# Three late scatter waits moved, the expert stage ordered by pairs of tiles, and the graph's feed-forward by pairs of tiles

## The chip, the cores and the metric

The kernel runs on one core of a Trainium2 chip. The time is device microseconds from launch to end, the median of 3 runs. The kernel before takes 2256.81 us (2252.81 to 2266.86).

## What is computed

Two layers of a graph network on 1,250 nodes of 512 features and 40,000 edges whose destinations are sorted. The parts that the change touches, cut to their core:

```python
dst = (1250 * uniform(40000) ** 2).astype(int32), sorted        # edges by destination
# graph attention over the edges (scores of every pair of nodes, weighted by a table of edges)
alpha = p / denom[src];  agg = segment_sum(alpha[:, :, None] * v[dst], src)
x = x + agg.reshape(n, C) @ Wo.T + bo
# the graph's feed-forward, 512 -> 1024 -> 512
z = layernorm(x, ln_ff_g, ln_ff_b)
x = x + silu(z @ W1.T + b1) @ W2.T + b2
...
# eight experts, 512 -> 256 -> 512 each, for every node, summed with softmax gates
hid = gelu(einsum('bnd,edf->bnef', y, W1) + b1)
out = einsum('bned,bne->bnd', einsum('bnef,efd->bned', hid, W2) + b2, gate)
```

All data is 32-bit float. A product with float operands shows as two matmul instructions in the trace: a product of 128 rows by 125 columns counts as x2 there.

## The kernel before

The nodes are cut into 10 tiles of 125. Each engine runs its own list of instructions in program order, written out by hand stage by stage (`gnn_...`, `att_...`, `ff_...`, `ffn_...`, `causal_...`, `expert_...`, `l1_...`, `last_...`), and waits on semaphores; a waiting instruction holds up all that stands behind it on its engine. `leave_stage` is a barrier of TensorE (PE), VectorE (DVE) and ScalarE (ACT).

**Edge table and attention.** POOL (GpSimd) scatters the edges into a table in HBM, 313 columns of 128 edges, one indirect DMA per column (L623), two in flight. The attention stage reads the table back in 50 blocks of 125 destinations by 250 sources into three buffers. Blocks 0 to 24 hold the destination tiles 0 to 4, blocks 25 to 49 the tiles 5 to 9: block 25 + 5g + n is destination tile 5 + n for the g-th group of sources. The DMA queue SP issues for each block i, in order: the count store of block i (L223 to adjacency, once ACT has copied the counts, `a_cc`), then the load of block i + 3 (six DMAs at L223 and L224, once DVE has used block i, `a_p`). Before the loads of blocks 25 to 27 it reads the number of scatter columns which the tiles up to that one need (`soon_filled`), and waits for them; before block 28 it waits for all 313 (`table_filled`). DVE multiplies every block by exponentials from ACT in two halves (L1488). The sums of these weights (L1524) are DVE's for blocks 0 to 24; for the later blocks they stand on POOL, behind all scatters. A half-block needs the sum of the half-block three before it, since it takes its buffer.

**Feed-forward (`ff_...`).** Per tile t: DVE normalizes into one buffer (`z`, L192), PE transposes it (`turn`, L198), ACT scales it into columns (`zT`, L1758, 4 activations), PE makes 32 products of 125 columns for the hidden layer (`hidden`, L1797), ACT takes Silu (L1774), PE makes 8 products of 512 columns for the output (`project`, L204, 16 instructions), DVE adds it to x (L1739). PE's order is turn(t + 2), hidden(t + 1), project(t). DVE's list, which the change leaves as it is: z(0), z(1), z(2), then for each tile t two adds (L1734, L1735), z(t + 3), a wait for project(t), the add at L1739, and the statistics of tile t - 1 (L172).

**Experts.** Per tile, PE makes 64 products of 125 columns (L2446) for all eight hidden layers of the next tile, then one bias product (L2473) and 8 x 2 products of 512 columns (L2488) for this tile; ACT takes Gelu of 125 columns at a time (L2413), DVE adds each expert's output times its gate to x (L2394).

Of the kernel before, what the change touches and what calls it, by code (L numbers as in the profile page):

```python
# [15 lines left out]
NODES = 1250  # L16
# [36 lines left out]
def gps_two_layers(nc, d):  # L53
# [11 lines left out]
    with ctx:  # L65
# [562 lines left out]
        SOON_KEYS = [float((SOON_TILES + w) * TP * NODES + 1) for w in range(4)]  # L628
# [776 lines left out]
        def att_sp(sp):  # L1405
# [299 lines left out]
        zT_f = [chunks(space.take(C)) for _ in range(2)]  # L1705
        hT_f = [chunks(space.take(8 * TP), TP, 8) for _ in range(2)]
# [42 lines left out]
        def ff_act(act):  # L1749
# [3 lines left out]
            def zT(t):  # L1753
                act.wait_ge(z_turned, Z_FF + t + 1)
                if t >= 2:
                    act.wait_ge(f_h, 2 * (t - 1))
                for k in range(KC):
                    last = nc.scalar.activation(zT_f[t % 2][:, k, :], bank(t % 2)[:, k * TP:(k + 1) * TP],  # L1758
                                                ACT.Identity, scale=lf_g[:, k:k + 1],
                                                bias=lf_g[:, KC + k:KC + k + 1])  # L1760
# [4 lines left out]
            for t in range(TILES):  # L1765
                if t + 2 < TILES:
                    zT(t + 2)
                if t >= 2:
                    act.wait_ge(f_o, t - 1)
                for a in range(2):  # L1770
                    n = 2 * t + a
                    act.wait_ge(f_h, n + 1)
                    for m in range(4):
                        last = nc.scalar.activation(hT_f[t % 2][:, 4 * a + m, :],  # L1774
                                                    bank(2 + n % 4)[:, m * TP:(m + 1) * TP], ACT.Silu,
                                                    bias=b1_g[:, 4 * a + m:4 * a + m + 1])
                    last.then_inc(f_s, 1)
            leave_stage(act, "ACT")

        def ff_pe(pe):  # L1780
# [8 lines left out]
            def hidden(t):  # L1789
                pe.wait_ge(z_cols, Z_FF + t + 1)  # L1790
                for a in range(2):
                    n = 2 * t + a
                    if n >= 4:
                        pe.wait_ge(f_s, n - 3)
                    for m in range(4):
# [1667 lines left out]
```

## Time and profile before

| | |
|---|---|
| median of 3 runs | 2256.81 us |
| the profiled execution: its time / its span | 2257.32 / 2255.5 us |
| PE busy in the span | 2059.9 us, 91% (DVE 60%, ACT 32%, POOL 32%) |
| chain that ended last, by engine | PE 59%, DVE 17%, DMA 9%, POOL 7%, ACT 4% |
| its lines | L204 17%, table scatters 8% and L623 7%, L2446 6%, L2488 6%, L1797 3% |
| attention from the first late block to its end | 786 to 1006 us |
| feed-forward | 1006 to 1167 us |
| experts | 1547 to 1850 us |

The chain is followed back from the last instruction; what stands in it was waited for. A stage is read by its own rows: who is busy there, who waits, and what ended the wait.

### The profile page before, as it was taken

To read this page: it belongs to the slowest core of one execution; us is meant where nothing else is said; L and a number is where in the kernel's file an instruction comes from. 1 tells how busy PE (TensorE), PEld (TensorE's weight loads), DVE (VectorE), ACT (ScalarE), POOL (GpSimd) and SP (SyncE) were. 2 spreads that over 40 slices of the span, in tenths; PEclk is the share of its full clock that TensorE was granted. 3 is DMA by queue.
4 is the path that set the end of the run, shared out by engine and by line. 5 is a ranking of instruction groups with operands and counts; after the bars stand their busy time and mean duration, and the time that the engine had idled before them with its cause. 6 is when DMAs were issued, how large, how long until landed. Compare 5 with 4: busy or idle time off the path is not lost.

```text
span 2255.5 us, 31449 instructions
## 1 busy us (share of the span) xinstructions
PE 2059.9 (91%) x11986; PEld 1259.6 (56%) x11986; DVE 1352.0 (60%) x3200; ACT 728.0 (32%) x1552; POOL 726.3 (32%) x508
## 2 busy tenths in 40 slices
PE   5998986999999878989999999999999999999977
PEld 3555554443345545547764467678666754455554
DVE  6665687988999967751224543431222243289997
ACT  4221122320035544422223355554111111135553
POOL 1346878887775565430000000000000000024442
PEclk9998998999999989999999999999999999999989
DMA  9995232223449977652000010004000013000000
GB/s 328 386 374 123 3 77 3 3 3 67 63 77 220 213 174 199 182 148 95 1 10 0 1 77 1 1 1 188 1 1 1 1 48 106 1 1 10 10 15 14
DMA packets 122055, 181.99 MB, mean 81 GB/s; under 512 B 67761, under 2 KB 69451, under 8 KB 118071
## 3 DMA queue, kind: packets, MB, share of 16 engines
q1 hardware_dynamic: 76833, 178.51, 25.2%
q0 software_dynamic: 45072, 1.46, 5.7%
q8 instruction: 96, 1.57, 0.3%
q14 instruction: 54, 0.44, 0.1%
HBM read 109.21 MB, written 70.71 MB: 80 GB/s over the span
## 4 chain that ended last, share of the span: by engine, by line
PE 59%; DVE 17%; DMA 9%; POOL 7%; ACT 4%; issue 3%; SPq 1%; DVEq 0%; PEldq 0%; ACTq 0%; POOLq 0%; PEld 0%
PE banks L204 17%; DMA edge_table<-arena 8%; POOL edge_table L623 7%; PE banks L2446 6%; PE banks L2488 6%; PE banks L1797 3%; PE banks L2274 2%; PE banks L2262 2%; PE banks L2249 2%; PE banks L2872 2%; PE banks L1593 2%; PE banks L2298 2%; PE banks L198 2%; PE banks L1614 1%; DVE arena L1488 1%
## 5 line engine op out<-in xcount | busy, mean ns | idle before, releaser
L623 POOL DMA_INDIRECT edge_table<-arena x313 | 521.3, 1666 | 269.4 <-DMA edge_table<-arena 164.5
L204 PE MATMUL banks<-arena 128*125 128x512 f32 x1200 | 550.4, 605 | 15.4 <-DVE arena L3092 14.3
L204 PEld LDWEIGHTS banks<-arena 128*125 128x125 f32 x1200 | 219.5, 191 | 258.2 <-issue 241.1
L2899 POOL CAST arena<-arena 125x128 f32<-125x128 uint32 x10 | 2.9, 290 | 699.3 <-DVE arena L3035 699.3
L1488 DVE TENSOR_TENSOR arena<-banks,arena 125x1000 f32<-125x1000 f32 x100 | 193.3, 1949 | 35.5 <-ACT banks L1567 26.9
L2394 DVE SCALAR_TENSOR_TENSOR arena<-banks,arena 125x512 f32<-125x512 f32 x80 | 60.1, 751 | 189.4 <-PE banks L2488 189.4
L2141 DVE CUSTOM_DVE_ANT_0 arena<-banks,arena 125x512 f32<-125x512 f32 (+8 forms) x144 | 73.0, 553 | 129.1 <-PE banks L2249 126.3
L1593 PE MATMUL banks<-arena 64*125 64x250 f32 x800 | 113.8, 403 | 38.6 <-DVE arena L1488 37.3
L2446 PEld LDWEIGHTS banks<-arena 128*128 128x128 f32 x1280 | 144.0, 192 | 6.7 <-issue 6.6
L2446 PE MATMUL banks<-arena 128*128 128x125 f32 x1280 | 146.4, 276 | 0.1
L1567 ACT ACTIVATE banks<-banks 125x1000 f32<-125x1000 f32 x100 | 99.0, 990 | 139.9 <-PE banks L1599 120.1
L2488 PE MATMUL banks<-arena 128*125 128x512 f32 x320 | 139.2, 593 | 0.0
L1524 POOL TENSOR_TENSOR arena<-arena 125x1000 f32<-125x1000 f32 x40 | 95.8, 2455 | 74.3 <-DVE arena L1488 74.2
L1593 PEld LDWEIGHTS banks<-arena 64*125 64x125 f32 x800 | 69.3, 187 | 79.9 <-DVE arena L1488 58.0
L1197 DVE TENSOR_REDUCE arena<-banks 125x2 f32<-125x1024 f32 (+1 forms) x120 | 112.2, 1029 | 0.0
L1311 PE MATMUL banks<-arena 64*125 64x512 f32 (+1 forms) x480 | 108.4, 555 | 4.0 <-DVE arena L1197 2.5
L2413 ACT ACTIVATE arena<-banks,arena 128x125 f32<-128x125 f32 x160 | 45.2, 369 | 203.1 <-PE banks L2446 203.1
L1614 PE MATMUL banks<-arena 125*64 125x250 f32 x800 | 108.8, 394 | 0.5 <-DVE arena L1488 0.5
L198 PE MATMUL banks<-arena 125*128 125x125 f32 x560 | 83.2, 280 | 23.1 <-DVE arena L753 6.9
L2107 POOL MEMSET arena<- 128x1250 f32 x1 | 1.1, 1140 | 315.9 <-PEq L148 315.9
L2488 PEld LDWEIGHTS banks<-arena 128*125 128x125 f32 x320 | 59.3, 188 | 74.0 <-issue 74.0
L198 PEld LDWEIGHTS banks<-arena 125*128 125x128 f32 x560 | 64.2, 145 | 54.5 <-issue 24.1
(374 smaller groups left out, 3405.9 us busy)
## 6 DMA issues: line engine op xcount, KB each, us to landing
edge_table<-arena SPq DMA_DIRECT2D x23, 2304.0 KB, 24.3
arena<-edge_table SPq DMA_DIRECT2D x100, 326.8 KB
arena<-edge_table SPq DMA_DIRECT2D x50, 330.8 KB
arena<-L_ffn_W SPq DMA_DIRECT2D x4, 2048.0 KB, 10.1
adjacency<-arena SPq DMA_DIRECT2D x50, 109.4 KB
arena<-adjacency SPq DMA_DIRECT2D x10, 546.9 KB
edge_table<-arena POOLq DMA_INDIRECT x313
arena<-edge_table SPq DMA_DIRECT2D x100, 37.9 KB
```

The lines of the kernel that those rows point to most:

```text
L198: last = nc.tensor.transpose(dst[:, k, :], src[:, k * 128:(k + 1) * 128], ident[0:TP, 0:TP])
L204: last = nc.tensor.matmul(dst, xT[:, i, :], w[:, i, 0:n], start=(i == 0), stop=(i == k - 1))
L623: pool.indirect_dma_start(d["table"], bass.IndirectOffsetOnAxis(ap=cell[0:EP, c:c + 1].bitcast(U32), axis=0), vals[0:EP, c * ROW:(c + 1) * ...
L1197: nc.vector.tensor_reduce(by_part_max[:, t, j, :, u % 3], unit_banks(u)[:, :, 0:b - a], AX_X, ALU.max).then_inc(g_mx, 1)
L1311: last = nc.tensor.matmul(unit_banks(u)[:, e, 0:b - a], qT_g[64 * e:64 * e + 64, j, tok(t)], kT_g[64 * e:64 * e + 64, j, a:b], start=True, ...
L1488: nc.vector.tensor_tensor(weights_of(m).rearrange("p (s e n) -> p s e n", s=2, e=2), unit_scores(m).rearrange("p e (s n) -> p s e n", s=2) ...
L1524: ops.tensor_tensor(total_p, total_p, weights_of(m), ALU.add).then_inc(a_sum, 1)
L1567: nc.scalar.activation(unit_scores(m), unit_scores(m), ACT.Exp).then_inc(a_e, 1)
L1593: nc.tensor.matmul(bank(at + e)[0:TP, CHUNK * s:CHUNK * (s + 1)], kT_g[64 * e:64 * e + 64, 2 * h + s, tok(b)], qT_g[64 * e:64 * e + 64, 2 ...
L1614: last = nc.tensor.matmul(bank(h)[64 * e:64 * e + 64, CHUNK * s:CHUNK * (s + 1)], V_g[0:TP, b, DH * head:DH * (head + 1)], weights_of(m)[: ...
L2446: last = nc.tensor.matmul(bank(2 + n % 3)[:, m * TP:(m + 1) * TP], w1_e[a // 2][:, k, (c % 8) * 128:(c % 8 + 1) * 128], yT[:, k, tok(t)], ...
L2488: last = nc.tensor.matmul(bank(5 + n % 3)[0:TP, :], hT_e[t % 2][:, 2 * e + c, :], w2_e[e // 4][:, 2 * (e % 4) + c, :], start=(c == 0), sto ...
```

## The change

It moves the scatter waits of the late table blocks: block 25 waits for the columns of tiles up to 6, block 26 for none of its own, block 27 for tiles up to 7, block 28 for tiles up to 8, block 29 for all. The feed-forward's hidden layer is made for two tiles at once, with products of 250 columns, in four parts of 8 products; the order of PE and ACT goes by pairs of tiles. The experts' hidden layer is made for one expert and two tiles at a time, seven such units ahead of the outputs; PE's and DVE's order goes by pair, expert, tile. Buffers follow.

```diff
-        SOON_KEYS = [float((SOON_TILES + w) * TP * NODES + 1) for w in range(4)]
+        SOON_UPTO = (SOON_TILES, SOON_TILES + 2, SOON_TILES + 3, SOON_TILES + 4)
+        SOON_KEYS = [float(n * TP * NODES + 1) for n in SOON_UPTO]
...
             def load_block(i):
                 c, b = chunk_and_tile(i)
-                late = i - BLOCKS // 2
-                if 0 <= late < len(SOON_KEYS) - 1:
-                    soon_filled(sp, late + 1)
-                if late == len(SOON_KEYS) - 1:
-                    table_filled(sp)
+                if i >= BLOCKS // 2 and c == 0:
+                    if b == TILES - 1:
+                        table_filled(sp)
+                    elif b in (SOON_TILES,) + SOON_UPTO[1:]:
+                        soon_filled(sp, 1 + sum(n <= b for n in SOON_UPTO[1:]))
...
         def ff_act(act):
-            for t in range(TILES):
-                if t + 2 < TILES:
-                    zT(t + 2)
...
+            for p in range(TILES // 2):
+                if p >= 2:
+                    act.wait_ge(f_o, 2 * (p - 1))
+                for a in range(4):
+                    n = 4 * p + a
                     act.wait_ge(f_h, n + 1)
...
                     last.then_inc(f_s, 1)
+                    if a < 2 and p + 1 < TILES // 2:
+                        zT(2 * p + 2 + a)
...
         def ff_pe(pe):
+            def hidden(p, a):
+                n = 4 * p + a
+                if a == 0:
+                    pe.wait_ge(z_cols, Z_FF + 2 * p + 2)
...
-            hidden(0)
-            for t in range(TILES):
-                if t + 2 < TILES:
-                    turn(t + 2)
-                if t + 1 < TILES:
-                    hidden(t + 1)
-                pe.wait_ge(f_s, 2 * t + 2)
-                if t >= 2:
-                    pe.wait_ge(f_x, t - 1)
-                project(bank(6 + t % 2)[0:TP, :], hT_f[t % 2], w2_g, k=8).then_inc(f_o, 1)
+            hidden(0, 0)
+            hidden(0, 1)
+            turn(2)
+            hidden(0, 2)
+            turn(3)
+            hidden(0, 3)
+            for p in range(TILES // 2):
+                more = p + 1 < TILES // 2
+                if more:
+                    for a in range(4):
+                        hidden(p + 1, a)
+                ff_out(2 * p)
+                if p + 2 < TILES // 2:
+                    turn(2 * p + 4)
+                ff_out(2 * p + 1)
+                if p + 2 < TILES // 2:
+                    turn(2 * p + 5)
...
         def expert_dve(dve):
+            dve.wait_ge(e_x, PAIR_ADDED * TILES // 2)
+            gather_stats(X, TILES - 2)
             leave_stage(dve, "DVE")
...
+        def expert_hidden(pe, n):
+            p, e = divmod(n, EXPERTS)
             if n >= 3:
                 pe.wait_ge(e_a, n - 2)
...
         def expert_pe(pe):
+            for n in range(HIDDENS):
+                p, e = divmod(n, EXPERTS)
+                if n + HIDDEN_AHEAD < HIDDENS:
+                    expert_hidden(pe, n + HIDDEN_AHEAD)
...
+                pe.wait_ge(e_a, n + 1)
+                for u in range(2):
+                    if e == 0:
+                        bias_rows_out(p, u)
```

Three places in the engines' order. First PE in the feed-forward, from the output of tile 0 on (L204 is the output of a tile, L198 the transposition of one, L1797 and now L1800 the hidden layer). Before:

```order
L204 MATMUL banks<-arena 125x512 [waits ff_silu_ready]
L204 MATMUL banks<-arena 125x512 x7
L198 MATMUL banks<-arena 128x125 [waits zT_ready,z_ready]
L198 MATMUL banks<-arena 128x125 x3
L1797 MATMUL banks<-arena 128x125 [waits ff_silu_ready,zT_ready]
L1797 MATMUL banks<-arena 128x125 x15
L1797 MATMUL banks<-arena 128x125 [waits ff_silu_ready]
L1797 MATMUL banks<-arena 128x125 x15
```

Now:

```order
L204 MATMUL banks<-arena 125x512 [waits ff_silu_ready]
L204 MATMUL banks<-arena 125x512 x7
L198 MATMUL banks<-arena 128x125 [waits zT_ready,z_ready]
L198 MATMUL banks<-arena 128x125 x3
L204 MATMUL banks<-arena 125x512 [waits ff_silu_ready]
L204 MATMUL banks<-arena 125x512 x7
L198 MATMUL banks<-arena 128x125 [waits zT_ready,z_ready]
L198 MATMUL banks<-arena 128x125 x3
L1800 MATMUL banks<-arena 128x250 [waits ff_silu_ready,zT_ready]
L1800 MATMUL banks<-arena 128x250 x7
```

The first transposition after the output of tile 0 was that of tile 3; it is now that of tile 4, and the one after the output of tile 1 is that of tile 5, right ahead of the hidden layer of tiles 4 and 5. Second, DVE in the feed-forward, from z(3) on, as it stands now; before it is the same with line numbers two lower (L1741 is the add that was L1739, L1736 and L1737 were L1734 and L1735):

```order
L192 TENSOR_SCALAR arena<-arena 125x512 [waits z_transposed,dve_step]
L1741 TENSOR_TENSOR arena<-banks,arena 125x512 [waits ff_out_ready]
L1736 TENSOR_TENSOR arena<-arena 125x512
L1737 TENSOR_TENSOR arena<-arena 125x512 [waits dve_step]
L192 TENSOR_SCALAR arena<-arena 125x512 [waits z_transposed,dve_step]
L1741 TENSOR_TENSOR arena<-banks,arena 125x512 [waits ff_out_ready]
L172 BN_STATS arena<-arena 125x6 [waits ff_added]
```

Nothing moved on DVE: the second L192 is z(4), and it stands behind the add that waits for the output of tile 0. Third, the queue SP from the count store of block 25 on, with the loads of blocks 28 and 29. Before:

```order
L223 DMA adjacency<-arena 112x2x125 [waits att_counts_copied]
L224 DMA adjacency<-arena 13x2x125
L223 DMA arena<-edge_table 112x756 [waits columns_scattered_1,columns_scattered_0,att_weights_ready]
L224 DMA arena<-edge_table 13x756
L223 DMA arena<-edge_table 112x747
L224 DMA arena<-edge_table 13x747
L223 DMA arena<-edge_table 112x747
L224 DMA arena<-edge_table 13x747
L223 DMA adjacency<-arena 112x2x125 [waits att_counts_copied]
L224 DMA adjacency<-arena 13x2x125
L223 DMA arena<-edge_table 112x756 [waits att_weights_ready]
```

Now, from the load of block 28 on:

```order
L223 DMA arena<-edge_table 112x756 [waits columns_scattered_1,columns_scattered_0]
L224 DMA arena<-edge_table 13x756
L223 DMA arena<-edge_table 112x747
L224 DMA arena<-edge_table 13x747
L223 DMA arena<-edge_table 112x747
L224 DMA arena<-edge_table 13x747
L223 DMA adjacency<-arena 112x2x125 [waits att_counts_copied]
L224 DMA adjacency<-arena 13x2x125
L223 DMA arena<-edge_table 112x756 [waits columns_scattered_1,columns_scattered_0,att_weights_ready]
```

Block 28's load waits for counts read from registers (four rows ahead of it), those of the tiles up to 8; the wait for all columns stood ahead of block 28 and stands now ahead of block 29.

## Rows read from the trace of the kernel before

**Rows 1.** windows view: stretch, PE, PEld, DVE, ACT, POOL busy us, PEclk, DMA share, GB/s

```profile
1021.90:1165.80 143.90, 143.84 (x832) 104.51 (x832) 28.43 (x48) 35.77 (x117) 0.00 (x0) 1.00 0.05 19
...
1600.70:1849.70 249.00, 248.17 (x1329) 169.94 (x1328) 65.67 (x90) 36.37 (x128) 0.00 (x0) 1.00 0.00 1
```

**Rows 2.** timeline of the DMA queue SP; start us, us, operation

```profile
801.67 0.32 SPq L223 DMA_DIRECT2D adjacency<-arena  x1
...
816.01 0.32 SPq L223 DMA_DIRECT2D arena<-edge_table  x1
```

**Rows 3.** timeline of POOL: scatters and first weight sums

```profile
771.59 1.54 POOL L623 DMA_INDIRECT edge_table<-arena  x1 [0.30 <-issue]
...
812.88 1.54 POOL L623 DMA_INDIRECT edge_table<-arena  x1 [0.33 <-issue]
813.88 9.62 POOL L1524 TENSOR_TENSOR arena<-arena 125x1000 f32<-125x1000 f32 x4
```

**Rows 4.** timeline of ACT: counts of block 28 copied; in brackets, idle before

```profile
822.67 0.65 ACT L1548 ACTIVATE arena<-arena 125x250 f32<-125x250 f32 x1 [12.96 <-DMA arena<-edge_table]
```

**Rows 5.** timeline of DVE: products of blocks 27 to 30

```profile
816.78 1.94 DVE L1488 TENSOR_TENSOR arena<-banks,arena 125x1000 f32<-125x1000 f32 x1 [7.00 <-POOL arena L1524]
824.43 3.79 DVE L1488 TENSOR_TENSOR arena<-banks,arena 125x1000 f32<-125x1000 f32 x2 [5.71 <-ACT banks L1567]
830.02 1.96 DVE L1488 TENSOR_TENSOR arena<-banks,arena 125x1000 f32<-125x1000 f32 x1 [1.80 <-ACT banks L1567]
...
836.80 1.97 DVE L1488 TENSOR_TENSOR arena<-banks,arena 125x1000 f32<-125x1000 f32 x1 [0.29 <-ACT banks L1567]
```

**Rows 6.** chain that ended last: first-layer products, and 256-column ones

```profile
1176.23 0.43 PE banks L198 x4
1176.66 3.46 PE banks L1894 x16
...
1044.22 7.15 PE banks L1797 x64
...
1600.78 14.49 PE banks L2446 x128
```

**Rows 7.** timeline of DVE in the feed-forward stage

```profile
1043.83 0.69 DVE L1739 TENSOR_TENSOR arena<-banks,arena 125x512 f32<-125x512 f32 x1 [13.39 <-PE banks L204]
...
1045.88 0.55 DVE L192 TENSOR_SCALAR arena<-arena 125x512 f32<-125x512 f32 x1
...
1060.92 0.55 DVE L192 TENSOR_SCALAR arena<-arena 125x512 f32<-125x512 f32 x1
```

**Rows 8.** timeline of PE in the feed-forward stage

```profile
1021.94 7.41 PE L1797 MATMUL banks<-arena 128*128 128x125 f32 x64 [0.36 <-ACT arena L1758]
...
1043.63 0.59 PE L198 MATMUL banks<-arena 125*128 125x125 f32 x4
...
1058.07 0.59 PE L198 MATMUL banks<-arena 125*128 125x125 f32 x4
```

**Rows 9.** timeline of ACT in the feed-forward stage

```profile
1020.38 2.89 ACT L1758 ACTIVATE arena<-banks,arena 128x125 f32<-128x125 f32 x8 [9.30 <-PE banks L198]
...
1044.26 1.50 ACT L1758 ACTIVATE arena<-banks,arena 128x125 f32<-128x125 f32 x4 [9.47 <-PE banks L198]
```

**Rows 10.** timeline of PE: the first products after three pauses (idle in brackets)

```profile
852.47 1.26 PE L1593 MATMUL banks<-arena 64*125 64x250 f32 x8 [2.38 <-DVE arena L1488]
...
891.60 1.11 PE L1593 MATMUL banks<-arena 64*125 64x250 f32 x8 [2.32 <-DVE arena L1488]
...
1011.84 8.02 PE L210 MATMUL banks<-arena 128*128 128x512 f32 x12 [5.07 <-DMA arena<-L_gnn_ln_ff_b]
```

**Rows 11.** windows view of the stretches after them, columns as in Rows 1

```profile
854.00:858.00 4.00, 4.00 (x20) 2.44 (x20) 1.60 (x3) 1.37 (x2) 3.50 (x2) 0.66 0.93 213
...
891.60:895.00 3.40, 3.40 (x26) 2.33 (x26) 2.88 (x2) 1.37 (x2) 3.37 (x2) 1.00 0.43 110
1011.80:1017.50 5.70, 5.66 (x7) 2.41 (x8) 0.90 (x4) 0.00 (x0) 0.00 (x0) 0.53 1.00 411
```

More of the change, by code:

```diff
@@ L1704, in gps_two_layers @@
         z_f = space.take(C)
-        zT_f = [chunks(space.take(C)) for _ in range(2)]
-        hT_f = [chunks(space.take(8 * TP), TP, 8) for _ in range(2)]
+        pair_rows = Space(2 * SLOT, 3 * SLOT)
+        zT_f = [chunks(place_of.take(KC * 2 * TP), 2 * TP) for place_of in (space, pair_rows)]
+        hT_f = [chunks(pair_rows.take(8 * 2 * TP), 2 * TP, 8) for _ in range(2)]
         f_h = sem("ff_hidden_ready")
@@ L1764, in ff_act @@
             zT(1)
-            for t in range(TILES):
-                if t + 2 < TILES:
-                    zT(t + 2)
[L1768 to L1771, printed above, removed]
+            for p in range(TILES // 2):
+                if p >= 2:
+                    act.wait_ge(f_o, 2 * (p - 1))
+                for a in range(4):
+                    n = 4 * p + a
                     act.wait_ge(f_h, n + 1)
[L1773 to L1776, printed above, removed]
+                    for m in range(2):
+                        c = 2 * a + m
+                        last = nc.scalar.activation(hT_f[p % 2][:, c, :], bank(2 + a)[:, 2 * TP * m:2 * TP * (m + 1)],
+                                                    ACT.Silu, bias=b1_g[:, c:c + 1])
                     last.then_inc(f_s, 1)
+                    if a < 2 and p + 1 < TILES // 2:
+                        zT(2 * p + 2 + a)
             leave_stage(act, "ACT")
@@ L2341, in gps_two_layers @@
         gateT = space.take(TILES * 128)
-        hT_e = [chunks(space.take(NH * TP), TP, NH) for _ in range(2)]
+        TWO = 2 * TP
+        HIDDEN_RING, HIDDEN_AHEAD = 8, 7
+        HIDDENS = TILES // 2 * EXPERTS
+        hT_e = [chunks(space.take(2 * TWO), TWO, 2) for _ in range(HIDDEN_RING)]
         EXPERT_END = BUF + 2 * KC * C + 1852
@@ L2385, in expert_dve, with biased @@
             dve.wait_ge(e_gate, 4)
-            for t in range(TILES):
-                x = X[0:TP, t, :]
+            def biased(p, u):
+                t = 2 * p + u
                 dve.wait_ge(e_b, t + 1)
-                nc.vector.tensor_tensor(x, bank(1)[0:TP, :], x, ALU.add).then_inc(e_x, 1)
-                for e in range(EXPERTS):
-                    n = (EXPERTS + 1) * t + e + 1
-                    dve.wait_ge(e_x, n)
-                    dve.wait_ge(e_o, EXPERTS * t + e + 1)
+                nc.vector.tensor_tensor(X[0:TP, t, :], bank(1)[0:TP, :], X[0:TP, t, :], ALU.add).then_inc(e_x, 1)
@@ L2404, in expert_act, with gelu @@
         def expert_act(act):
-            def gelu(t, a):
-                if a == 0 and t >= 2:
-                    act.wait_ge(e_o, EXPERTS * (t - 1))
-                n = NH // 4 * t + a
+            def gelu(n):
+                e = n % EXPERTS
+                if n >= HIDDEN_RING:
+                    act.wait_ge(e_o, 2 * (n - HIDDEN_RING) + 2)
                 act.wait_ge(e_h, n + 1)
-                for m in range(4):
-                    c = 4 * a + m
-                    last = nc.scalar.activation(hT_e[t % 2][:, c, :], bank(2 + n % 3)[:, m * TP:(m + 1) * TP],
-                                                ACT.Gelu_apprx_tanh, bias=b1_e[:, c:c + 1])
+                for c in range(2):
+                    last = nc.scalar.activation(hT_e[n % HIDDEN_RING][:, c, :], bank(2 + n % 3)[:, c * TWO:(c + 1) * TWO],
+                                                ACT.Gelu_apprx_tanh, bias=b1_e[:, 2 * e + c:2 * e + c + 1])
```

131 lines of the change are left out of this document (71 added, 60 removed).

## The prediction

> **What bounds the kernel now.** I read the page first. PE is busy in 91% of the span and carries 59% of the chain that ended last, so a change in PE's work counts where PE is full, and a wait on PE costs its whole length there. Then the windows view, for the stages that the change touches [rows 1]: in the feed-forward PE is busy 143.84 of 143.90 us and in the experts 248.17 of 249.00 us, both at the full clock (2.4 GHz). There is no wait to remove in either; they can gain only by less PE time, and lose by any wait that a new order makes. The third place is the attention around 802 to 836 us, where PE does wait; I read it engine by engine [rows 2 to 5].
>
> **The scatter wait.** SP stores the counts of block 25 at 801.67 and loads block 28 only at 816.01 [rows 2]; between, it waits for the last scatter, issued at 812.88 [rows 3]. ACT sits idle 12.96 us until the block has landed [rows 4], and DVE's first product with it starts at 824.43 [rows 5]. Which column does block 28 need? The destinations are 1250 u², so 40000 x sqrt(1125/1250) = 37,947 edges lie in tiles 0 to 8: 297 columns of 128, or 298, as they are counted in pairs. POOL issued the 298th at 771.59 [rows 3]; the last one was waited for some 3 us after its issue, and even three times that is long past by 801.67. So block 28 is loaded at about 804 (I allow 2 us for the store and the register reads). Block 25's new wait, for the 262 columns of tiles 0 to 6, costs nothing: its load stands three blocks, some 18 us, ahead of block 28's turn at 801.67, when the 298th column was out already, and the 262nd long before.
>
> Late next is block 29: the load that waits for all columns goes out at 816.01, as block 28's did. Block 28 is to be multiplied while that is on its way. But a second limit stands there: POOL makes the late weight sums, and it starts them at 813.88, after the last scatter, four in 9.62 us [rows 3]; DVE's second half of block 27 waited 7.00 us for the first of them [rows 5]. Block 28's halves need the second and third, at 818.7 and 821.1, so they just fit ahead of 824.4. From there the sequence is the old one moved by a block. In the old one that distance is 5.6 us (824.43 to 830.02) or 6.8 (830.02 to 836.80) [rows 5]. I take **-6**; ends -3 (the sums and a low clock take half of it) and -7.
>
> **First-layer products.** A 125-column instruction takes 7.15/64 = 0.1117 us in the feed-forward and 14.49/128 = 0.1132 in the experts; a 256-column one 3.46/16 = 0.2163 [rows 6]. Six columns fewer at 256 columns to 213 ns make 0.2112 for 250. The feed-forward has 640 instructions of 125 (ten tiles of 64), then 320 of 250: 71.5 to 67.6, **-3.9**. The experts have 1280, then 640: 144.9 to 135.2, **-9.7**. In the 250-column form no row of this kernel stands on a full array; the ends are this and nothing gained (2 x 0.113 = 0.226 each), and the 256-column row is by far the nearest.
>
> **The experts' order.** PE's order keeps every wait covered as far as I can follow it. A unit is 16 x 0.2112 = 3.4 us of hidden layer and 3.4 us of outputs. Its buffer of hidden values is free one unit earlier, Gelu has had four units of time, and DVE's two adds fit in 6.8 us. The cover that hides the second bias product of a pair is the first expert's output, 1.7 us, against about 0.9 for the bias add that it waits for. At the end DVE takes the statistics of tile 8 behind the last add, which it did earlier before: that row costs 0.6, the difference between z(4) and z(5) below, and I take 0.7. Experts in all **-9.0**.
>
> **The feed-forward's order.** Here waits are made. PE now transposes tile 4 right behind the output of tile 0, but z(4) stands on DVE behind the add that waits for that very output. In the old trace the same DVE chain can be timed. Output 0 ends and its add starts at 1043.83; z(4) ends at 1045.88 + 0.55 = 1046.43 [rows 7]. PE had gone on at 1043.63 with another tile's transposition [rows 8]; now it must stand until 1046.48, 2.85 us. For the next tiles DVE has the statistics in between: PE went on at 1058.07 [rows 8], z(5) ended at 1061.47 [rows 7], so 3.45 us. This happens at six transpositions, of tiles 4 to 9: 2.85 + 5 x 3.45 = 20.1. The old order had turn(4) behind output 1, one tile later, and so no wait.
>
> Three of these (tiles 5, 7, 9) stand directly ahead of a hidden layer that needs them. A transposition started at 1043.63 [rows 8], ACT's columns were done at 1044.26 + 1.50 = 1045.76 [rows 9], PE can go on at 1045.86, 2.23 later, of which the transposition itself takes 0.43 [rows 6]: 1.8 each, 5.4. At the start the hidden layer now needs two tiles of columns, ready at 1020.38 + 2.89 = 1023.27 [rows 9] rather than 1021.94 [rows 8]: 1.4. Sum: -3.9 + 20.1 + 5.4 + 1.4 = **+23.0**; ends +19 (if 0.4 of each of the ten waits overlaps other work) and +25.
>
> The Trainium skill, Perfetto Trace Analysis, section Optimizing Tensor Performance, says that larger matmuls are more efficient than smaller ones where they can be had. The rows agree for the products by themselves; by the rule alone the feed-forward would take 2.5 us less, by the rows of DVE it takes 23 more, since the order that goes with the larger products exposes DVE.
>
> **The clock.** A pause can throw PE's clock to the lower of its two levels (1.2 and 2.4 GHz). After 5.07 us of idling [rows 10] the granted clock was 0.53 over 5.7 us [rows 11], so nearly all of it at half speed: 5.7 x 0.47 = 2.7 us lost. After 2.38 us it was 0.66 over 4 us, 1.4 lost; after 2.32 us it stayed at 1.00 [rows 10, 11]. The feed-forward gets three pauses of 5.7 us broken only by a transposition, and three of about 3. The lower end is no fall, the upper six falls at 2.7. I take three falls at 1.4: **+4**.
>
> **Sum.** 2257.3 - 6 + 23.0 + 4 - 9.0 = 2269.3, against the profiled execution's own 2257.32, which is 0.5 above the median.
>
> **The rivals.**
> 1. PE falls to the low clock at all six pauses, at 2.7 each: +16.2 in place of +4, 2281.5, slower by 1.07%. It decides from 14.6 us of loss on (1% of 2257, 22.6, less the other terms, +8). For it: the pause of 5.07 us did cost 2.7, and all six new pauses are longer than the 2.38 us that once sufficed [rows 10, 11]. Against: the fall after the short pause cost half as much, and a pause of 2.32 us passed without one.
> The Trainium skill, TensorE: Matmul & The Clock Gate, section HAM oscillation — how this bites in real kernels, tells of a loop whose waits throw the clock down at every turn. By it this rival holds; [rows 11] show both outcomes.
> 2. The feed-forward does not wait, since DVE is only 28.43 us busy there [rows 1]: then 2257.3 - 6 - 2.5 - 9.0 = 2239.8, 0.8% faster. Against it: DVE's list is in program order, and the wait for the output stands ahead of z.
> 3. The scatter change gives nothing, because POOL's sums are what DVE waits for: 2275.3.
> 4. Products of 250 columns gain nothing over two of 125: 2269.3 + 3.9 + 9.7 = 2283, slower.
>
> **How the numbers follow.** Forecast 0.66, rival 1 0.12, rival 2 0.07, rival 3 0.10, rival 4 0.05. The time is the forecast's, 2269. The range 2256 to 2284 holds the forecast with its ends (-7 to -3, +19 to +25, clock 0 to 10), rival 3 and the near part of rivals 1 and 4; it leaves out rival 2 and the far ends, under 0.2 in all. About 1% (22.6 us) is what a measurement of this kernel can tell from no change: faster 0.04 (rival 2 with a better attention), slower 0.14 (rivals 1 and 4, both close above the bound), same 0.82.
>
> **What would show it.** In the new profile block 28 is loaded near 804 and block 29 near 816, and the attention ends some 6 us earlier. The feed-forward, first hidden product to last add, takes about 171 us rather than 144, with PE idle some 25 us and six gaps of about 3 us put down to DVE ahead of transpositions (L198) and three of 1.8 put down to ACT. The experts take about 9 us less with PE as full as before and 0.211 us per 250-column instruction. I am wrong if the transpositions follow the outputs without a gap, if gaps appear among the experts, or if the clock holds through the pauses or falls at each.

## The result and the profile after

The changed kernel takes 2290.83 us (2287.35 to 2297.15, 4 runs) against 2254.81 for the kernel before beside it: a ratio of 1.0153, interval 1.0127 to 1.0178. Run again in a later set beside a fresh kernel before it took 2285.19 against 2253.15, ratio 1.0152 (1.0137 to 1.0168). It is slower, by 32 to 36 us, where 2269 was forecast with a range up to 2284.

The whole difference of the two profiled executions can be read off by cutting both at the same instructions. The last column is the same kernel's profile from the later set; the column before it is what the prediction's terms say for that stretch.

| stretch | before | after | difference | forecast | after, second profile |
|---|---|---|---|---|---|
| start to the last scatter's issue | 812.88 | 819.96 | +7.08 | 0 | 812.35 |
| to the end of the attention's last denominator product | 184.36 | 177.98 | -6.38 | -6 | 177.99 |
| to the first hidden product of the feed-forward | 24.70 | 26.00 | +1.30 | +1.4 | 26.34 |
| feed-forward, to its last add | 144.64 | 176.59 | +31.95 | +25.6 | 179.68 |
| to the first hidden product of the experts | 380.63 | 385.47 | +4.84 | 0 | 385.45 |
| experts, to their last output product | 301.65 | 293.68 | -7.97 | -9.7 | 293.69 |
| to the last product of all | 402.71 | 403.28 | +0.57 | +0.7 | 403.29 |
| sum | 2251.57 | 2282.96 | +31.39 | +12 | 2278.79 |

Three rows miss by more than 2 us: the scatters, the feed-forward, and the stretch behind it.

The windows view of the changed kernel, columns as in Rows 1: the feed-forward, the 6.6 us behind it, and the experts. It is to be read beside [rows 1].

```profile
1023.94:1200.53 176.59, 151.92 (x512) 100.25 (x512) 27.72 (x48) 28.60 (x73) 0.00 (x0) 0.93 0.03 14
1200.53:1207.17 6.64, 5.96 (x33) 5.96 (x33) 3.83 (x23) 1.71 (x3) 0.00 (x0) 0.63 0.01 2
1586.00:1879.68 293.68, 293.57 (x1049) 189.56 (x1048) 73.20 (x104) 39.69 (x90) 0.00 (x0) 1.00 0.06 22
```

The feed-forward is no longer full: 24.7 of its 176.59 us are idle, and the granted clock, 1.00 before, is 0.93. PE's busy time is 151.92 us, 8.1 more than before, although its products have become cheaper. The experts are as full as before.

PE's waits in the feed-forward of the changed kernel: line, what it waited for, us in total, times, longest.

```profile
PE banks L198 <- DVE arena L192: 19.1, 6, 3.3
PE banks L1800 <- ACT arena L1761: 6.5, 4, 1.7
```

These are the six gaps at transpositions, and the gaps at hidden layers: three of 1.59 inside the stage and one of 1.75 at its start, which the table's third row holds. The timeline of PE shows the first three, at the transpositions of tiles 4 and 5 and at the hidden layer behind; it is to be read beside [rows 8].

```profile
1063.36 0.65 PE L198 MATMUL banks<-arena 125*128 125x125 f32 x4 [2.69 <-DVE arena L192]
1063.84 7.03 PE L204 MATMUL banks<-arena 128*125 128x512 f32 x16
1074.15 0.65 PE L198 MATMUL banks<-arena 125*128 125x125 f32 x4 [3.28 <-DVE arena L192]
1076.39 3.82 PE L1800 MATMUL banks<-arena 128*128 128x250 f32 x10 [1.59 <-ACT arena L1761]
```

And DVE's list between output 1 and the transposition of tile 5, to be read beside [rows 7]: the add of the output that PE has just made, the statistics and two adds behind it, and only then z.

```profile
1070.91 0.69 DVE L1741 TENSOR_TENSOR arena<-banks,arena 125x512 f32<-125x512 f32 x1 [7.61 <-PE banks L204]
...
1073.55 0.55 DVE L192 TENSOR_SCALAR arena<-arena 125x512 f32<-125x512 f32 x1
```

z starts 2.64 us after the add and ends at 1074.10; PE goes on at 1074.15.

The windows view behind each of the six transpositions, and in the stage behind the feed-forward, called the router here (L1880 to L1911, products of weights); the third number from the right is the granted clock.

```profile
1063.40:1070.90 7.50, 7.47 (x20) 3.26 (x20) 0.00 (x0) 2.22 (x6) 0.00 (x0) 1.00 0.00 0
1074.10:1080.30 6.20, 4.56 (x16) 3.75 (x17) 0.00 (x0) 2.93 (x8) 0.00 (x0) 0.72 0.00 0
1101.70:1108.70 7.00, 6.94 (x20) 3.30 (x20) 0.01 (x1) 2.22 (x6) 0.00 (x0) 1.00 0.00 0
1112.50:1121.50 9.00, 7.35 (x23) 6.02 (x24) 0.00 (x1) 3.20 (x9) 0.00 (x0) 0.62 0.01 2
1141.40:1145.40 4.00, 3.97 (x10) 2.20 (x10) 0.00 (x0) 2.22 (x6) 0.00 (x0) 0.65 0.00 0
1153.50:1162.50 9.00, 7.35 (x23) 6.04 (x24) 0.01 (x1) 3.22 (x9) 0.00 (x0) 0.62 0.01 2
1203.00:1213.50 10.50, 10.50 (x39) 9.27 (x39) 3.17 (x17) 1.71 (x3) 0.00 (x0) 0.55 0.00 1
```

PE drops to 1.2 GHz behind four of the six, behind all three double pauses and one of the single ones, and runs nearly the whole of this stretch of the router at that level. In the same view of before the stretch 1171 to 1180 stands at 0.82:

```profile
1171.00:1180.00 9.00, 9.00 (x38) 7.68 (x39) 3.44 (x17) 1.72 (x5) 0.00 (x0) 0.82 0.01 3
```

The next lines are the changed kernel's stretches at the low clock inside the feed-forward, cut at their ends, with their sum: one at the start of the stage and these four. The last line is a stretch far behind, 12 us ahead of the experts, where before stands at 1.00.

```profile
1024.72:1028.13 3.41, 3.41 (x10) 2.78 (x9) 0.00 (x0) 0.47 (x1) 0.00 (x0) 0.50 1.01 423
1075.92:1079.33 3.41, 2.94 (x7) 2.47 (x8) 0.00 (x0) 1.85 (x6) 0.00 (x0) 0.50 0.00 0
1113.47:1120.29 6.82, 5.50 (x13) 4.55 (x14) 0.00 (x0) 2.71 (x8) 0.00 (x0) 0.50 0.01 2
1140.77:1144.19 3.42, 2.76 (x7) 1.72 (x8) 0.57 (x2) 1.63 (x5) 0.00 (x0) 0.50 0.00 0
1154.43:1161.25 6.82, 5.45 (x13) 4.50 (x14) 0.00 (x0) 2.76 (x8) 0.00 (x0) 0.50 0.01 2
sum 23.88, PE 20.06 PEld 16.02 DVE 0.57 ACT 9.42 POOL 0.00; mean PE 4.01 PEld 3.20 DVE 0.11 ACT 1.88 POOL 0.00
...
1570.85:1574.26 3.41, 3.38 (x17) 3.41 (x17) 0.00 (x0) 1.74 (x4) 0.00 (x0) 0.50 1.01 432
```

PE is busy for 20.06 us at half speed inside the feed-forward, so the clock costs 10.0 us there.

The attention, in three timelines of the changed kernel, to be read beside [rows 2, 3, 5]. SP loads block 28 at 803.86, as forecast, and block 29 at 823.10:

```profile
803.86 0.32 SPq L223 DMA_DIRECT2D arena<-edge_table  x1
...
823.10 0.32 SPq L223 DMA_DIRECT2D arena<-edge_table  x1
```

POOL, however, issues its last scatter at 819.96, and DVE waits 14.18 us for the sums that stand behind it on POOL:

```profile
810.73 1.54 POOL L623 DMA_INDIRECT edge_table<-arena  x1 [2.39 <-DMA edge_table<-arena]
...
819.96 1.54 POOL L623 DMA_INDIRECT edge_table<-arena  x1 [0.30 <-issue]
```

```profile
823.86 1.94 DVE L1489 TENSOR_TENSOR arena<-banks,arena 125x1000 f32<-125x1000 f32 x1 [14.18 <-POOL arena L1525]
...
829.47 1.98 DVE L1489 TENSOR_TENSOR arena<-banks,arena 125x1000 f32<-125x1000 f32 x1 [1.35 <-ACT banks L1568]
```

### The profile page after: what moved, and what is told of

Read it like the earlier page. It is cut to its first block, busy times and chain, and to the rows that moved or that the text cites. A ratio compares the mean times of both kernels' runs of the same rounds, so it can differ in the third digit from the quotient of the medians.

```text
span 2286.9 us, 29385 instructions
## 1 busy us (share of the span) xinstructions
PE 2062.5 (90%) x11026; PEld 1235.7 (54%) x11026; DVE 1351.1 (59%) x3200; ACT 709.4 (31%) x1432; POOL 728.3 (32%) x508
## 3 DMA queue, kind: packets, MB, share of 16 engines
q1 hardware_dynamic: 76833, 178.51, 24.7%
## 4 chain that ended last, share of the span: by engine, by line
PE 58%; DVE 18%; DMA 9%; POOL 6%; ACT 4%; issue 3%; SPq 1%; DVEq 0%; PEldq 0%; ACTq 0%; POOLq 0%; PEld 0%
PE banks L204 17%; DMA edge_table<-arena 8%; PE banks L2532 6%; PE banks L2483 6%; POOL edge_table L623 6%; PE banks L1800 3%; PE banks L2291 2%; PE banks L2279 2%; PE banks L2266 2%; PE banks L2916 2%; PE banks L2315 2%; PE banks L1594 2%; PE banks L198 2%; PE banks L1615 2%; DVE arena L1489 1%
## 5 line engine op out<-in xcount | busy, mean ns | idle before, releaser
L204 PE MATMUL banks<-arena 128*125 128x512 f32 x1200 | 550.9, 606 | 15.5 <-DVE arena L3136 14.4
L204 PEld LDWEIGHTS banks<-arena 128*125 128x125 f32 x1200 | 220.5, 191 | 260.0 <-issue 242.6
L2483 PE MATMUL banks<-arena 128*128 128x250 f32 x640 | 141.6, 374 | 0.1
L2483 PEld LDWEIGHTS banks<-arena 128*128 128x128 f32 x640 | 120.4, 189 | 28.5 <-issue 15.7
L198 PE MATMUL banks<-arena 125*128 125x125 f32 x560 | 84.1, 282 | 42.1 <-DVE arena L192 20.5
L198 PEld LDWEIGHTS banks<-arena 125*128 125x128 f32 x560 | 64.2, 146 | 74.9 <-DVE arena L192 26.3
L2451 ACT ACTIVATE arena<-banks,arena 128x250 f32<-128x250 f32 x80 | 33.0, 466 | 206.0 <-PE banks L2483 205.9
```

The source lines that it names most:

```text
L198: last = nc.tensor.transpose(dst[:, k, :], src[:, k * 128:(k + 1) * 128], ident[0:TP, 0:TP])
L204: last = nc.tensor.matmul(dst, xT[:, i, :], w[:, i, 0:n], start=(i == 0), stop=(i == k - 1))
L2483: last = nc.tensor.matmul(bank(2 + n % 3)[:, c * TWO:(c + 1) * TWO], w1_e[e // 4][:, k, at:at + 128], yT[:, k, tok(2 * p, 2)], start=(k == ...
```

## The experiments

**One part alone.** Three kernels hold one part of the change each: the two pieces of the scatter wait; the three of the feed-forward; the four of the experts.

> Only the feed-forward is changed. In the full change it took 176.59 us from the first hidden product to the last add (before 143.95): 19.1 us of waiting at six transpositions, 4.8 at three hidden layers, and 151.92 us of TensorE work that before took 143.84 at the full clock; the granted clock fell five times in it, and for 10.2 us in the router behind it. Theory A (waits as forecast, but the clock falls at nearly each of them): 176 here again, five or six falls, the whole 33 to 36 us longer, ratio 1.015 to 1.016. Theory B (the clock's falls are a matter of the single execution, three on the average): waits the same 24, two or three falls, 27 to 30 us longer.

Measured: 2292.71 us against 2254.59, ratio 1.0159 (1.012 to 1.0197). Its feed-forward, windows view:

```profile
1021.50:1198.09 176.59, 151.93 (x512) 100.20 (x512) 27.72 (x48) 28.60 (x73) 0.00 (x0) 0.93 0.03 13
```

This is Theory A. The waits are the same to 0.1 us, the work is the same, and the stage lasts 176.59 us again; the stretch to the experts is 385.48. The feed-forward alone makes the whole loss, and in this execution the clock falls at the same places as in the first profile.

> Only the expert stage is changed. In the full change, from its first hidden product to its last output it took 293.68 us (1586.00 to 1879.68), before 301.65 (1547.21 to 1848.86). Theory A (the products of 250 columns give it by themselves): 293.7 here, 8 us less in all, ratio 0.9965. Theory B (the stage's gain is lost again behind it, or the clock falls at its entry as at 1571.9 in the full change): 293 to 295 in the stage, but the time lower by 5 or less.

Measured: 2249.34 us, ratio 0.997 (0.9953 to 0.9987); the stage takes 293.68 us. Theory A is the nearer one: the experts give 8.0 us in their stage, and over the runs the whole time is 6.8 lower by the ratio. The interval, 2.9 to 10.6 us, does not exclude Theory B's 5 or less.

> Only the scatter wait is changed. In the profiled run of the full change the last scatter was issued at 819.96 us, in that of before at 812.88; from the last scatter's issue to the end of the attention's last denominator product it was 177.98 us, before 184.36. Theory A (the wait's change is worth 6.4 us from the last scatter on, and when the last scatter comes is a matter of the single execution): that stretch is 178 again here, the last scatter falls somewhere between 812 and 821, and over several rounds the time is 6 us lower than before (ratio 0.997). Theory B (the earlier load of block 28 delays the scatters by the 7 us that it gains): the last scatter is near 820 again, the scatters before 300 us are as late as in the full change, and the time is that of before (ratio 1.000). Theory C (DVE waits for the sums on GpSimd in any case): the stretch is 184 and the ratio 1.000.

Measured: 2252.19 us, ratio 0.9988 (0.997 to 1.0006): no difference that these runs can tell from none, nor from -6. In its profile the last scatter goes at 815.26 and the last denominator product ends 178.14 us later (timelines of POOL and of PE):

```profile
807.82 1.54 POOL L623 DMA_INDIRECT edge_table<-arena  x1 [2.37 <-DMA edge_table<-arena]
...
815.26 1.54 POOL L623 DMA_INDIRECT edge_table<-arena  x1 [0.37 <-issue]
```

```profile
992.29 1.11 PE L1654 MATMUL banks<-arena 128*128 128x250 f32 x4 [0.41 <-DVE arena L1464]
```

Theory C falls: from the last scatter on the change is worth 6.2 us. In the ten profiles of kernels with the new wait that stretch is 176.9 to 180.0 us, in the three with the old one 184.3 to 185.0. When the last scatter comes differs by more than that gain from profile to profile: 807.98 to 820.73 with the new wait (mean 815.2), 811.36 to 816.22 with the old (mean 813.5). The lateness in the first profile was there long before the change acts: the 101st scatter of the changed kernel went at 331.72, that of before at 323.93. Theory B falls as a cause of the 7 us; a smaller form of it stays open (below).

**VectorE's list.** z one tile further ahead, TensorE's order unchanged:

```diff
-                if t + 3 < TILES:
-                    z(t + 3)
+                for n in (3, 4) if t == 0 else (t + 4,):
+                    if n < TILES:
+                        z(n)
                 dve.wait_ge(f_o, t + 1)
```

> The full change, but VectorE makes the normalized rows z one tile further ahead, so that they no longer stand behind the add that waits for the very output; TensorE's order is unchanged. Theory A (the six gaps are VectorE's order): the waits at the transpositions fall from 19.1 us to under 2, the three waits of 1.6 for ScalarE's columns stay (4.8), and the clock decides the rest: if pauses of 1.6 to 2 us leave it up, the feed-forward takes 140 + 5 = 145 and the time is 32 us below that of the full change, near 2258; if it falls at each of the three, 1.7 each, 150 and near 2263. Rival (TensorE waits for something else there as well): the gaps stay above 1.5 us each and the time is within 15 us of 2290.

Measured: 2254.7 us, ratio 0.9991 (0.9972 to 1.0011). Waits and windows view of its feed-forward, with the stretch behind its first remaining pause:

```profile
PE banks L1801 <- ACT arena L1762: 6.5, 4, 1.7
```

```profile
1019.10:1167.12 148.02, 142.47 (x512) 94.88 (x512) 27.72 (x48) 28.55 (x73) 0.00 (x0) 0.99 0.04 17
...
1065.10:1072.00 6.90, 6.86 (x32) 6.17 (x33) 1.22 (x2) 2.25 (x6) 0.00 (x0) 1.00 0.00 0
```

This is Theory A in its better form, though 3 us above the 145 expected, since the fall of the clock at the start stays (see the run on the start below). The six gaps are gone, the three of 1.6 stay, and behind them the clock stays at 1.00. One edit in DVE's list takes 28.6 us out of the stage: 19.1 of waits and 9.5 of PE's busy time. PE's instructions and their order are the same, so the 9.5 go with the pauses: 8.3 by the four falls that are gone, the rest with the six gaps themselves.

**The transposition's place.** z two tiles ahead (3, 4, 5 at first, then t + 5), and each transposition one output earlier:

```diff
+                if p + 2 < TILES // 2:
+                    turn(2 * p + 4)
                 ff_out(2 * p)
                 if p + 2 < TILES // 2:
-                    turn(2 * p + 4)
+                    turn(2 * p + 5)
                 ff_out(2 * p + 1)
-                if p + 2 < TILES // 2:
-                    turn(2 * p + 5)
```

> The full change, but VectorE makes the normalized rows z two tiles further ahead than in the full change, and TensorE transposes each of the tiles 4 to 9 one output earlier. With z one tile ahead alone the feed-forward took 148.02 us (before 143.95), with three waits of 1.6 for ScalarE's columns left and one fall of the clock at its start. Theory A (these three waits are the transposition's place alone): no wait in the feed-forward behind its first product, 143.2 us, 4.8 less than with z ahead alone, the time 2248 to 2250, ratio to before 0.997 to 0.998. Rival (the earlier transpositions make ScalarE's columns stand ahead of the SiLU of the same pair, and the outputs wait for that): new gaps at the outputs of 1 us or more, 148 or above.

Measured: 2251.62 us against 2257.44, ratio 0.9966 (0.9951 to 0.9982).

```profile
1023.62:1166.09 142.47, 141.68 (x512) 94.82 (x512) 27.73 (x48) 28.60 (x73) 0.00 (x0) 0.99 0.04 16
```

This is Theory A: no wait is left inside the stage, which is 2.2 us shorter than before's 144.64. The time is 1.6 us above the expected range, the ratio a little below it, since the kernel before beside it was slower too. The stretch from the feed-forward to the experts is 385.49, as in the changed kernel, though the pauses are gone: so how low the clock stands behind the feed-forward does not follow from those pauses alone.

**Pauses filled.** The waits stay, and PE does unread products in them. In the first size 13 products of 512 columns (`FILL_Z`) stood ahead of each of the six transpositions and 6 ahead of each of three hidden layers:

```diff
             def turn(t):
-                pe.wait_ge(z_rows, Z_FF + t + 1)
                 if t >= 2:
                     pe.wait_ge(z_cols, Z_FF + t - 1)
+                if t >= 4:
+                    unused_products(bank(t % 2), w2_g[:, 0, :], FILL_Z)
+                pe.wait_ge(z_rows, Z_FF + t + 1)
...
```

> The full change, but TensorE does products whose results nobody reads in the pauses that the new order makes: 13 of 512 columns (2.8 us) ahead of each of the six transpositions and 6 (1.3 us) ahead of each of three hidden layers. The waits themselves stay. In the full change the feed-forward took 176.59 us, of which TensorE worked 151.92; at the full clock its work would be 140. Theory A (12 us of the feed-forward and 2.6 behind it are the clock's, which falls because TensorE pauses): no fall in the feed-forward but for the one at its start (near 1024), 165 us from the first hidden product to the last add, the time 12 to 15 us below that of the full change, 2276 to 2279. Theory B (TensorE is slower there for another reason, such as what the new products read): the feed-forward stays near 176 and the time near 2290. Theory C (the added products are in the way by themselves): more than 176.

Measured: 2331.76 us, ratio 1.0317 (1.0295 to 1.0339). This is Theory C: I had sized the products wrong. The 96 products lengthen the stage from mended's 142.47 to 224.88, so one takes 0.86 us, not the 0.21 I had reckoned. PE never pauses behind the first product, and the stage's granted clock is 0.99, but the products take far more time than the pauses did.

> As in the run filled, but with the right size: one of its unread products of 512 columns took 0.87 us, not 0.21, so the 96 of them made 83 us and the feed-forward 224.88. Here the six pauses ahead of transpositions hold 6 unread products of 256 columns each (6 x 0.435 = 2.6 us) and the three ahead of hidden layers 3 each (1.3 us); the waits behind them stay. Theory A (12 us are the clock's): no fall in the feed-forward but the one at its start, 165 to 167 us (140 of work, 24 of waits, 1.7 for the fall) in place of 176.59; the time 9 to 15 us below that of the full change beside it. Theory B (the clock falls all the same, or TensorE is slow for another reason): 174 or more.

Measured: 2276.12 us, ratio 1.0111 (1.0094 to 1.0127), beside 1.0152 for the changed kernel in the same set. Windows view and waits:

```profile
1016.93:1185.36 168.43, 163.21 (x602) 111.14 (x602) 27.72 (x48) 28.60 (x73) 0.00 (x0) 0.99 0.04 15
```

```profile
PE banks L198 <- DVE arena L192: 3.5, 5, 0.7
PE banks L1806 <- ACT arena L1761: 2.6, 4, 1.7
```

This is Theory A, 1.4 us over its range. The dependences on DVE and ACT are all there and PE gets nothing useful done in them, yet the kernel is 9.1 us faster than the changed kernel beside it. In the two profiles it gains 11.3 us in the stage (179.68 there) and 3.3 behind it (382.20 against 385.45); a scatter chain that ends 2.0 later and 3.1 more in the last stages take some of it back. The 14.5 us come from the clock: the five falls behind the start cost the changed kernel 11.5 us in that profile (after_again, below), and here none of them is left.

**The start.** Mended, with three unread products of 256 columns ahead of the first hidden layer:

```diff
             turn(1)
+            unused_products(bank(2)[:, 0:C // 2], w2_g[:, 0, 0:C // 2], 3)
             hidden(0, 0)
```

> The run mended, and three unread products of 256 columns (1.3 us) in the wait of 1.7 us ahead of the first hidden layer. In mended the feed-forward took 142.47 us with one fall of the clock of 3.4 us at its start (1025.1), and 10.2 us at the lower clock behind it (1168.4). Theory A (the fall at the start follows from that wait): no fall there, the feed-forward takes 140.5 to 141, the time 2 us below that of mended, ratio 0.9955 to 0.996. Theory B (it follows from the longer pause ahead of it, 4.8 us at 1007): the fall stays, and so does the time, ratio 0.9966.

Measured: 2243.4 us against 2253.15, ratio 0.9962 (0.9949 to 0.9975). This is Theory A:

```profile
1015.52:1156.31 140.79, 139.99 (x512) 93.55 (x512) 27.73 (x48) 28.56 (x73) 0.00 (x0) 1.00 0.04 17
```

The pause of 1.7 us at the start cost 1.7 more by the clock. This stage at the full clock and without a pause behind its first product is also the measure for the others: the same 512 instructions take 139.99 us of PE here, 151.92 in the changed kernel's first profile and 155.00 in its second, 11.9 and 15.0 more. Of these the clock is 10.0 and 13.2 (half of PE's time at the low clock); the other 1.9 goes with the nine pauses themselves (z_ahead, with three pauses and the fall at the start alone, has 2.5 more, of which the fall is 1.7). The kernel beats both before and after.

**The change without its feed-forward.**

> The full change without its feed-forward: the scatter wait and the experts of the full change, the feed-forward of before. The two alone gave ratios of 0.9988 (0.997 to 1.0006) and 0.997 (0.9953 to 0.9987). If they add up and the clock plays no part: 0.9958, some 9.5 us below before; from the last scatter to the last denominator product 178 us, the experts 293.7, the feed-forward 144.64. Rival (the scatter wait's gain goes where the scatters come later, the rest is the experts'): 0.997. With the old wait the time from the 257th to the last scatter was 165.2, 159.8 and 161.6 us, with the new one 161.9 to 166.2 in six runs; here it is expected between 160 and 166.

Measured: 2244.01 us, ratio 0.9968 (0.9946 to 0.9989): the rival's figure, though the interval holds both. From the last scatter (807.98) to the last denominator product it is 178.32 us, the experts 293.68, the feed-forward 144.65: these parts stand as forecast. The last stages, however, took 406.42 us, 3.72 more than before: 0.7 at the experts' end and the rest mostly at the low clock behind the experts (0.50 from 1856.40 to 1863.23). With the new order of the experts this stretch took 403.3 us in four profiles, 404.7 in two and 406.4 in three, with the old one 402.6 to 402.7 in four, so a part of the experts' gain can be lost behind them. Whether the whole gain arrives over several executions these runs don't decide: the medians differ by 9.1 us, the ratio says 7.2.

**POOL's sums.** With the scatter wait alone, the late weight sums of blocks 25 to 29 moved to DVE:

```diff
-        DVE_PASSES = CHUNKS
+        DVE_PASSES = CHUNKS + 1
```

> The scatter wait's change alone, and VectorE instead of GpSimd adds up the weights of blocks 25 to 29 in the second pass. In the run with the scatter wait's change alone TensorE waited for VectorE's weights for 24.9 us in all between 800 and 1000 us (12.2 at the longest), since VectorE's second half of block 27 waits for sums that stand on GpSimd behind the last scatter; from the last scatter's issue to the last denominator product it was 178.14 us. Theory A (GpSimd's sums are the limit left): block 27 and block 28 are multiplied while the scatters still go on, the stretch falls to 170 to 174 us and the time is 4 to 8 us below that of the scatter wait's change alone. Theory B (the last block's load behind the last scatter is the limit left): the stretch stays within 2 us of 178 and so does the time.

Measured: 2258.16 us against 2257.44, ratio 0.9997 (0.9978 to 1.0015). Timeline of DVE:

```profile
817.05 1.20 DVE L1525 TENSOR_TENSOR arena<-arena 125x1000 f32<-125x1000 f32 x1
826.25 1.93 DVE L1489 TENSOR_TENSOR arena<-banks,arena 125x1000 f32<-125x1000 f32 x1 [8.00 <-ACT banks L1568]
```

This is Theory B. DVE is through with block 28 at 818 and then waits for block 29; the stretch is 177.61. GpSimd's sums, which the prediction called the second limit, cost nothing on balance: the last block's load does, and it stands behind the last scatter.

**The changed kernel once more.**

> The full change again, beside the runs above, for its feed-forward and for when its last scatter comes. If the feed-forward's pauses throw the clock down in each execution alike: 176.6 us again, with five falls, ratio 1.014 to 1.016. If it is a matter of the execution: another number of falls. The last scatter: 819.96 in the first profile; if its lateness is chance, anywhere from 811 to 821, and 178 us from there to the last denominator product.

Measured: the ratio above, 1.0152, the last scatter at 812.35, the same waits of 19.1 and 6.5 us, and one fall of the clock more than in the first profile:

```profile
1016.68:1196.36 179.68, 155.00 (x512) 102.07 (x512) 27.74 (x48) 28.57 (x73) 0.00 (x0) 0.91 0.03 12
...
1095.66:1099.07 3.41, 3.04 (x7) 1.89 (x8) 0.32 (x1) 1.90 (x6) 0.00 (x0) 0.50 0.02 5
```

The additional fall is behind the third transposition (second line), after a single pause of 3.28 us that passed without one in the first profile (the window 1101.70:1108.70 above). PE's time at the low clock in the whole stage is 26.35 us here, so the clock costs 13.2, of which 1.7 at the start.

## Why the prediction missed

**Right: the feed-forward's waits.** Forecast 20.1 us at six transpositions and 5.4 at three hidden layers, measured 19.1 and 4.8; the start 1.4, measured 1.3. z_ahead shows that it is DVE's list and nothing else, mended that the rest is the transposition's place. Rival 2 (no waits) is out.

**Right: the products of 250 columns.** Forecast 0.2112 us each. (The prediction missed that before has such products on a full array, 40 at L1653 in groups of four, of which the later ones start 0.211 us apart; they bear the price out.) The chain that ended last has the changed kernel's experts as

```profile
1634.70 3.37 PE banks L2483 x16
1638.07 3.43 PE banks L2532 x8
...
1678.91 1.05 PE banks L2512 x2
1679.96 1.91 PE banks L2532 x4
```

so 0.2106. In the feed-forward the gain is 143.84 - 139.99 = 3.85, forecast 3.9. Rival 4 is out.

**Mis-sized: the experts' old products.** The stage gave 7.97 us where 9.7 was forecast. The forecast took 0.1132 us for an old product from a row of 128 in 14.49 us [rows 6], and that row stands right behind a bias product (L2473), as the chain of before shows:

```profile
1599.73 1.05 PE banks L2473 x2
```

At the feed-forward's 0.1117 us, 128 such instructions take 14.30. The difference of 0.19 us is what the work right behind a bias product takes more, and four output products behind one now take 0.19 more as well: 1.91 us rather than 1.72 (half of 3.43). So this cost moved from the hidden layer to the outputs, and the forecast booked it, 1.9 us for 1280 instructions, as a gain. At 0.1117 the forecast would have been 7.8.

**Wrong: the clock, the term "+4".** This is the step that carried the answer to the wrong side of 1%. I took three falls at 1.4 us from two rows of before, the one fall after 2.38 us and none after 2.32 [rows 10, 11]. Measured were four falls in one profile and five in the other, at 2.1 to 2.3 us each, besides one at the start of 1.7: 10.0 and 13.2 us. On the way to the experts 4.84 us more came, for which I had nothing: 3.1 in the router, which starts at the low clock, and 1.7 in the stretch at 1570.85, whose cause stays open. Together 15 to 18 us in place of 4, and 1.9 of PE's busy time that goes with the nine pauses themselves, which I had at nothing. Rival 1 (six falls, +16.2) came near in the number of falls, and by luck in the sum, since a quarter to a third of what was lost came behind the stage. What misled me was to price pauses one by one: each second pause comes as two (3.28, a short transposition, 1.59), and behind a double pause the clock fell every time in both profiles, six of six; behind single ones of 2.69 to 3.29 us it fell three times in six. The Trainium skill, TensorE: Matmul & The Clock Gate, section HAM oscillation — how this bites in real kernels, describes a loop whose waits throw the clock down at every turn; the changed kernel's rows agree for the double pauses.

**Wrong in what it brought: the scatter wait, the term "-6".** The mechanism held to 0.4 us: block 28 is loaded at 803.86 and everything behind the last scatter is 6.38 us shorter. But I made the sum from the start of the program, as if the last scatter came at the same time in each execution. That chain of 313 scatters is paced by DMA round trips, and its end moved by 13 us among ten profiles; in the first profile of the changed kernel it was 7.08 late and took the whole gain. For that profile rival 3 (the scatter change gives nothing) had this term right, with the wrong mechanism.

Open: over the runs the scatter wait's change seems worth less than 6 us (2.7 by its ratio alone, with an interval from 6.8 less to 1.4 more). In the first profile one more scatter stalls behind the earlier load of block 28, the one at 810.73 with 2.39 us above; in before the last such stall is at 805.48:

```profile
805.48 1.54 POOL L623 DMA_INDIRECT edge_table<-arena  x1 [2.67 <-DMA edge_table<-arena]
807.33 1.54 POOL L623 DMA_INDIRECT edge_table<-arena  x1 [0.30 <-issue]
```

A stall of that size would give back a third of the gain. But the time from the 257th to the last scatter overlaps between the kernels (159.1 to 166.2 us with the new wait, 159.8 to 165.2 with the old), so this is argued, not shown.

**The sum with the measured sizes**, against the first profile: +7.1 - 6.4 + 1.3 (scatters, attention, start), +23.9 of waits, -3.9 of products, +10.0 of clock and +1.9 that go with the pauses themselves in the feed-forward, +4.8 of clock behind it, -8.0 + 0.6 for the experts: +31.3, where the cut shows +31.39.

## What to carry to other kernels

When an edit puts a consumer right behind its own producer on a full engine (here a transposition behind the very output that VectorE's list waits for), move the input ahead on the other engine's list before anything else: one line of that list was worth 28.6 us. Price a pause of TensorE as its length and the work behind it at half speed, and expect most of it where two pauses stand close together; here 24 us of waits brought 10 to 13 us of clock in the stage, and up to 5 were lost behind it. Read a product's price from a row that doesn't stand behind a product of another kind. A gain behind a chain that DMA round trips pace is measured from that chain's end, and the time from the start needs several executions.

## What the runs showed of the hardware

- Two pauses of 3.28 and 1.59 us with a transposition between were followed by 1.2 GHz in six of six cases of the changed kernel's two profiles, single ones of 2.69 to 3.29 us in three of six; the same pause at the same place differed between two executions. Three pauses of 1.6 us alone (z_ahead) were followed by it in none, but the pause of 1.7 us at the stage's start in each of the seven profiles that have it, and no more when products filled it (mended_start): a pause's length alone doesn't decide.
- The same pause of 1.48 us between the feed-forward and the router is followed by more or less of the low clock: the stretch from the last add to the experts took 380.5 to 380.6 us in five profiles, 382.2 in three, 385.5 in four, with the same instructions of PE. The four also have a second stretch at 0.50 some 12 us ahead of the experts, worth 1.7 of their 4.9 us. One profile took 391.1 (experts_only), with 20.5 us at 0.50 from 1310.43 on.
- An unread product of 512 columns is two instructions and took 0.86 us, so a filler has to be sized by its own row.
- Four output products behind a bias product (8 rows on the array) took 1.91 us, four behind other products 1.72; 128 hidden products of 125 columns behind one took 14.49 us, 14.30 at the price of the feed-forward's.
